# TensorE's values product put ahead of the transposes in each slot of a two-layer cross-attention kernel

## What is computed

```python
a = _layer_norm(audio_kv, ln_gamma, ln_beta)          # (8, 1500, 256)
Q = (hidden_states @ Wq.T).reshape(B, Tt, HEADS, HEAD_DIM).transpose(0, 2, 1, 3)
K = (a @ Wk.T).reshape(B, Ta, HEADS, HEAD_DIM).transpose(0, 2, 1, 3)
V = (a @ Wv.T).reshape(B, Ta, HEADS, HEAD_DIM).transpose(0, 2, 1, 3)
scores = jnp.einsum('bhtd,bhsd->bhts', Q, K) * scale
attn = jax.nn.softmax(scores, axis=-1)
out = jnp.einsum('bhts,bhsd->bhtd', attn, V)
```

## Time and profile before

| | |
|---|---|
| median of 3 runs | 1822.67 us (1819.48, 1822.67, 1823.98) |
| profiled execution's own time | 1822.74 us |
| its span, first to last instruction | 1820.9 us |
| mean granted TensorE clock (share of full speed) | 0.973 |
| first layer's slots | from about 60 us to 483 us |
| steady period of a batch of the first layer | 50.2 to 51.7 us |
| busy share of the span | PE 92%, DVE 67%, ACT 57%, POOL 49% |

### The profile page before, as it was taken

One profiled execution on the slowest core, in us unless ns is written; L12 is line 12 of the kernel. 1 busy time (PEld: TensorE's weight loads), 2 busy tenths in 40 slices (PEclk: granted clock), 3 DMA queues, 4 the chain that ended last, 5 costly groups with the idle time before them and its releaser, 6 DMA issues.

```text
span 1820.9 us, 40621 instructions
## 1 busy us (share of the span) xinstructions
PE 1671.2 (92%) x12520; PEld 1571.5 (86%) x12520; DVE 1214.3 (67%) x2334; ACT 1041.7 (57%) x2023; POOL 898.0 (49%) x655
## 2 busy tenths in 40 slices
PE   3698889887798999999999999989999999999997
PEld 2577777776688999999999997789999999999986
DVE  5477777766546667667766767466676676677673
ACT  2476666656454566565655656545565665656563
POOL 4455555533234365355445547544554653554483
PEclk8899999999889999999999999999999999999998
DMA  7766676775322111001101104221111010010021
GB/s 228 210 146 166 157 178 175 175 171 118 90 64 81 43 34 67 34 34 67 35 33 67 49 23 140 64 78 35 57 58 43 34 67 34 34 67 0 1 88 42
DMA packets 109911, 149.69 MB, mean 82 GB/s; under 512 B 25540, under 2 KB 95684, under 8 KB 109828
## 3 DMA queue, kind: packets, MB, share of 16 engines
q1 hardware_dynamic: 108484, 142.45, 28.0%
q10 hardware_dynamic: 1344, 6.19, 1.0%
HBM read 108.32 MB, written 3.42 MB: 61 GB/s over the span
## 4 chain that ended last, share of the span: by engine, by line
PE 63%; DVE 9%; SPq 6%; issue 4%; ACT 3%; DMA 2%; POOL 2%; DVEq 0%; ACTq 0%; POOLq 0%
PE ps L765 11%; PE ps L767 11%; PE ps L766 11%; PE ps L1016 7%; PE ps L1020 7%; PE ps L1018 7%; SPq L389 4%; PE ps L951 2%; DMA q<-q_scratch 2%; DVE ar L1851 1%; PE ps L996 1%; PE ps L983 1%; SPq L392 1%; DVE negm L1879 1%; ACT prob L1292 1%
## 5 line engine op out<-in xcount | busy, mean ns | idle before, releaser
L717 POOL TENSOR_TENSOR rr<-ar,rr 125x512 fp32r<-125x512 f32 x336 | 450.8, 1376 | 417.1 <-ACT rr L1474 401.1
L1016 PE MATMUL ps<-cx,rr 125*128 125x258 f32 x1344 | 395.5, 294 | 0.0
L1020 PE MATMUL ps<-cx,rr 125*128 125x258 f32 x1344 | 379.3, 282 | 0.0
L1018 PE MATMUL ps<-cx,rr 125*128 125x256 f32 x1344 | 379.2, 282 | 0.0
L765 PE MATMUL ps<-rr,ct 128*125 128x256 f32 x1152 | 330.6, 287 | 4.5 <-DVE ar L1896 2.7
L767 PE MATMUL ps<-rr,ct 128*125 128x256 f32 x1152 | 325.2, 282 | 0.0
L766 PE MATMUL ps<-rr,ct 128*125 128x256 f32 x1152 | 324.9, 282 | 0.0
L1018 PEld LDWEIGHTS ps<-cx,rr 125*128 125x128 f32 x1344 | 254.7, 190 | 0.0
L1020 PEld LDWEIGHTS ps<-cx,rr 125*128 125x128 f32 x1344 | 254.7, 190 | 0.0
L1016 PEld LDWEIGHTS ps<-cx,rr 125*128 125x128 f32 x1344 | 253.6, 189 | 0.1
L1461 ACT ACTIVATE ar<-ar 125x512 f32<-125x512 f32 x336 | 208.6, 626 | 78.2 <-DVE ar L1896 54.5
(11 more groups left out here) (210 smaller groups left out, 3743.2 us busy)
## 6 DMA issues: line engine op xcount, KB each, us to landing
raw_t<-in_ctx_t SPq DMA_DIRECT2D x24, 1500.0 KB, 6.3
k<-khl SPq DMA_DIRECT2D x192, 187.5 KB
raw<-in_ctx SPq DMA_DIRECT2D x16, 1500.0 KB
raw<-in_ctx SPq DMA_DIRECT2D x8, 1408.0 KB
raw<-stat_scratch ACTq DMA_DIRECT2D x7, 750.0 KB, 3.9
w_raw<-in_wq SPq DMA_DIRECT2D x32, 128.0 KB, 2.3
w_raw<-in_wk SPq DMA_DIRECT2D x32, 128.0 KB, 2.2
qo<-in_wqt SPq DMA_DIRECT2D x32, 128.0 KB, 2.4
```

Source lines behind the costliest of these rows:

```text
L717: pool.tensor_tensor(group(p[:, 1, :, :], u, k), x, f(group(p[:, 0, :, :], u, k)), ALU.subtract)\
L1016: pe.matmul(ps[:, bank, 0:D + 2], hi, cx[0:KC, c, 0:D + 2], start=c == 0, stop=False, skip_group_check=True)
L1018: pe.matmul(ps[:, bank, 0:D], hi, cx[0:KC, c, D + 2:CW], start=False, stop=False, skip_group_check=True)
L1020: mm = pe.matmul(ps[:, bank, 0:D + 2], lo, cx[0:KC, c, 0:D + 2], start=False, stop=c == CH - 1, skip_group_check=True)
```

## The change

In TensorE's `slot` the values block (step 7) goes ahead of the eight transposes (step 5) and of the statistics' transpose (step 6). The order becomes: scores, last third of the transposes, keys, weighted sum, **values, transposes, statistics**. Its waits move with it. No instruction is added or removed, and no other engine's stream changes.

```diff
                     weighted(b if t else b - 1, (t - 1) % SLOTS, g - 1, n if t else 1 - n)
-                transposes(g, t, 0)
-                transposes(g, t, 1)
-                if t == 3 and kind == "full":
-                    pe.wait_ge(s["zoc"], g)
-                    turn_stats(b + 2)
                 if t in V_AT and kind != "plain":
                     u = V_AT[t]
                     pe.wait_ge(s["zvl"], 6 * (b + 1) + u)
                     if t == 6 and later:
                         pe.wait_ge(s["zre"], b)
                     values(b + 1, u, 6)
+                transposes(g, t, 0)
+                transposes(g, t, 1)
+                if t == 3 and kind == "full":
+                    pe.wait_ge(s["zoc"], g)
+                    turn_stats(b + 2)
                 if t == 4 and later:
```

## The result

| | before | after |
|---|---|---|
| median of 17 runs | 1823.33 us | 1831.63 us |
| ratio, with its 95% interval | | 1.0045 (1.0028 to 1.0063) |
| profiled execution's own time, its span | 1822.74, 1820.9 us | 1832.52, 1830.7 us |
| mean granted TensorE clock | 0.973 | 0.971 |
| first layer ends (start of its output product) | 485.94 us | 493.82 us |

The change makes the kernel 8.3 us slower, by the medians. The forecast was 1831.0 us, 8.4 above the 1822.67 us that it started from.

What follows compares the result with a forecast made beforehand. TensorE, busy 88% of a first-layer batch, bounds beside a GpSimd and SP ring. Slot 3's -1.19 us and exposed waits sum to +1.68 a batch, +6.0 over five; with clock and later slots +8.4: 1831.0 us, range 1819 to 1838.

Steps and rivals of the forecast that it cites:

- The statistics' wait: Slot 3: the statistics' transpose no longer waits for GpSimd's power; 7.61 instead of 8.80 us, -1.19 us per full batch.
- The exposed chain: Slots 0, 1, 2: transposes, high split, low splits lose their cover; row maximum to row maximum 6.64 us: +0.72, +0.60, +0.42.
- second ring: Slots 0 to 2: the ring over bank 3, which the first low split frees for the next four transposes; 6.39 us.
- a 0.45 us wait of the four transposes: Sign in the profile after: in slots 0, 1, 2 and 7 the four transposes wait about 0.45 us for a low split.
- Slot 7: Slot 7: high split delayed behind ScalarE's rounding of the context; 6.88 us against 5.92, +0.96.
- Slots 4 and 5: Slot 4: weighted sum ends later, +0.48 us; slot 5: today's idle goes, -0.31 us.
- Five periods: Slot (0, 4) to (5, 4): five batches of 51.99 us, 259.95 instead of 253.93 us, +6.0.
- The cover in batch 6: Slots (5, 4) to (6, 4): ScalarE's 7.16 us idle for key copies swallows a 2.6 us loss; priced nothing.
- the clock's half: Five periods: half of the 1.55 us lost to a lower-clock stretch, added as 0.8 us because it may return.
- The gain wins: Rival: slots 7, 0, 1, 2 stay at 5.9 us, GpSimd's ring sets a 48.8 us period; 1815 us, chance 8%.
- It cancels: Rival: the exposed wait is about half of what was summed; 1824 us (1819 to 1828), chance 20%.
- The clock falls more often: Rival: TensorE's gaps in every slot bring the lower clock in every period; 1838 us, chance 12%.

Runs made afterwards that it cites:

- experiment 1: From the kernel before: values block ahead of the transposes in slot 3 alone, old order elsewhere; ratio 0.9971, median 1816.99 us.
- experiment 3: From the kernel before: only the statistics' transpose with its wait moved behind slot 3's values block; ratio 0.9959, median 1816.88 us.
- experiment 4: From the changed kernel: values block between the first four and second four transposes, statistics behind; ratio to the kernel before 1.0005, median 1824.80 us.
- experiment 5: From the changed kernel: VectorE's row maximum over one of three blocks of 500 scores; ratio to the kernel before 0.9953.
- experiment 6: From the kernel before: VectorE's row maximum over one of three blocks of 500 scores; ratio 1.0021.
- experiment 7: The kernel of experiment 3 with VectorE's row maximum over one of three blocks of 500 scores; ratio to the kernel before 0.995.
- 8: The kernel of experiment 3 with slot 6's values block ahead of its weighted sum; ratio to the kernel before 0.9932, median 1813.61 us.
- 2: From the kernel before: values ahead of the transposes in every slot with values but slot 3; ratio 1.0052, median 1834.15 us.

## Why the prediction was right, point by point

- **The statistics' wait.** Forecast: slot (4, 3) from 8.80 to 7.61 us, no wait at L775. Measured 7.62, no wait; in the others of batches 1 to 5 7.47 to 7.80. Experiments 1 and 3 show the gain by itself.
- **The exposed chain.** Forecast 6.64 us for slots 0, 1 and 2, from 0.58 + 0.58 + 1.16 behind the eight transposes; measured 6.67, 6.82, 6.66, with the same 0.58 and 0.58 in the rows above. Experiment 4 was worked out by the same pieces (6.4, measured 6.35). The second ring's 6.39 is seen in experiment 5 as 6.33. The forecast of a 0.45 us wait of the four transposes was half right: they start 0.47 later, but the bracket shows 0.23, because the tail of the scores (to 337.28) covers the rest.
- **Slot (4, 1)** is 0.18 us longer than forecast, and so is slot 1 of batches 1 to 3 (6.82 to 6.84); in batches 0, 5 and 6 it takes 6.65 to 6.67. In slot (4, 1) the values' first weights are loaded 0.22 us after the end of the split that they wait for, and the values start 0.25 after it:
```profile
294.52 0.68 DVE L1658 TENSOR_TENSOR v<-ps,v 128x512 fp32r<-128x512 f32 x1
...
295.12 2.05 DVE L1664 BATCH_NORM_STATS2 bn<-raw 128x6 f32<-128x256 f32 x6
295.42 0.19 PEld L765 LDWEIGHTS ps<-wv_s,ct 128*128 128x128 f32 x1 [0.29 <-issue]
```
  In slot (5, 1) the load comes 0.06 us after the split (347.45 against 347.39), as forecast, and VectorE's statistics run there too, so they are not the reason. What differs is the program around it: `whole_batches` runs batches 1 to 4 in a loop and has the others written out. In slot (4, 1) the trace has two of TensorE's waiting instructions between the split's end and the load (at 295.25 and 295.34); in slot (5, 1) such a one stands before the split's end, at 346.96. No run here was made for it.
- **Slot 7** was over-priced: 6.88 against 6.69. ScalarE's context block holds the high split back to 2.61 us into the slot (332.28 - 329.67), not 2.8, and the low split starts at 3.19, hardly later than the row maximum lets it.
- **Slots 4 and 5.** 5.58 and 5.15 against 5.64 and 5.33: the gain in slot 5 was put at 0.31 and is 0.13, over five periods the largest miss.
- **Slips in the working**, none of which moves the forecast by more than 0.3 us: slot 7's surplus is 3.38 - 3.16 = 0.22, not 0.24; its 0.58 + 0.95 + 1.97 make 3.50, not 3.4; and slots (5, 7) to (6, 2) lose 2.7 by the terms given, not 2.6.
- **Five periods**: 259.95 against 260.83 us. That they are so near is in part luck: over the five, slot 5 costs 1.1 us and slot 1 0.7 us more than forecast, slot 7 1.0 and slot 6 0.6 less.
- **The cover in batch 6.** From slot (5, 4) to (6, 4) 55.63 us instead of the earlier trace rows's 56.32, and ScalarE's idle time before the late keys falls from the 7.16 us of the earlier trace rows:
```profile
417.19 0.59 ACT L1238 ACTIVATE kst<-ps 128x500 f32<-128x500 f32 x1 [5.88 <-POOL khl L574]
```
  So the slots' loss there was hidden, as priced; the stretch is even 0.7 us shorter, which offsets most of the 0.9 us that the five periods take above the forecast. Why it is shorter was not looked into.
- **The sum.** The first layer ends 7.88 us later; the forecast without the clock's half was 7.6. The clock's 0.8 is not seen in the first layer. The profiled spans differ by 9.8 us, the medians by 8.3. At the second layer's LayerNorm near 1140 us the kernel after is 7.45 us behind (1147.77 against 1140.32), some 20 us later 9.83 us (1169.05 against 1159.22): there the clock is granted lower for longer. By stretch, 14 us of it, first in the kernel before, then in the kernel after:
```profile
1146.00:1160.00 14.00, 12.53 (x59) 10.94 (x59) 5.83 (x9) 4.75 (x8) 1.85 (x3) 0.76 0.06 17
```
```profile
1153.50:1167.50 14.00, 13.21 (x50) 11.68 (x51) 4.83 (x8) 3.35 (x6) 2.32 (x2) 0.58 0.00 1
```
  The change moves no instruction there; why the clock differs is open. So the total of 8.4 met the 8.3 by luck in its last 0.8 us: the term for the clock stands for no event of the changed kernel's first layer.
- **The rivals.** "The gain wins" needed four slots at 5.9 us; none is. That its ring exists is shown by experiments 3, 6 and 7. "It cancels" falls with the 6.67. "The clock falls more often": the profile after has full clock in all five periods. The new gaps in slots 0 to 2 are 0.2 to 0.3 us; slots 6 and 7 keep waits of 1.3 to 1.4 us, which did not bring it down there. The mean clock of the 17 executions after has a median of 0.973, the same as the profile before. In experiments 6 and 7 the clock fell behind waits of 1.7 to 4.2 us. The Trainium skill, "TensorE: Matmul & The Clock Gate", section "HAM oscillation — how this bites in real kernels", says that waits between bursts of matmuls bring the clock back to half. Its case has waits longer than the bursts between them. Experiments 6 and 7 agree in kind. The prediction's "by that rule this rival would hold" took the rule further, to gaps that are a small part of a slot, and the full clock behind gaps of 0.2 to 0.3 us does not bear it out. Why experiment 4 lost the clock in three slots 6 and the changed kernel in none is open.

## What to carry to other kernels

A block of independent matmuls is a cover, and moving it uncovers what it hid: before moving it, list what runs on the other engines during it, and add those durations behind the instruction that will now stand last. If one wait is to be covered, move the waiting instruction behind the cover (experiment 3, ratio 0.9959), not the cover ahead of everything (1.0045); the cover ahead in the one slot that waits (experiment 1, 0.9971) exposes one slot only and can't be told from experiment 3. Where two rings turn side by side, what one engine saves comes back as waits as soon as the other ring binds (experiment 6).

## What the hardware showed that was not expected

- After TensorE had waited 3.39 us in slot (3, 3) of experiment 6, its matmuls of 256 columns followed one another at 0.21 us instead of 0.12; the values block lost 1.2 us on top of the wait.
- The length of the wait alone does not decide. The stretch at the lower clock that the earlier trace rows show in one period lies in slot (1, 6). In order of time, the kernel before:
```profile
167.86 0.98 PE L864 MATMUL ps<-pt,v 128*66 128x224 f32 x4 [1.35 <-DVE pt L1658]
168.64 1.70 PE L847 MATMUL ps<-ident,prob 112*128 112x112 f32 x8
...
321.01 0.60 PE L864 MATMUL ps<-pt,v 128*66 128x224 f32 x4 [1.35 <-DVE pt L1658]
321.45 0.93 PE L847 MATMUL ps<-ident,prob 112*128 112x112 f32 x8
```
  Behind the same wait of 1.35 us the eight transposes last 1.70 us in slot (1, 6) and 0.93 in slot (4, 6). By stretch, the same kernel:
```profile
168.00:172.00 4.00, 4.00 (x24) 4.00 (x25) 1.67 (x4) 3.30 (x7) 1.15 (x3) 0.60 0.91 188
172.00:176.00 4.00, 2.77 (x24) 2.39 (x24) 2.85 (x3) 3.03 (x4) 4.00 (x2) 1.00 0.72 148
```
  The granted clock is 0.60 of full over the first 4 us, so most of them ran at the lower of its two levels, 1.2 GHz of 2.4, while TensorE worked throughout; it is full again in the next 4 us.
- Experiment 7 shows the same with longer waits. Its statistics' transposes in slots (2, 3) and (4, 3):
```profile
203.27 0.28 PE L775 MATMUL ps<-ident,mv 128*12 128x128 f32 x1 [1.69 <-POOL mv L580]
...
304.88 0.28 PE L775 MATMUL ps<-ident,mv 128*12 128x128 f32 x1 [2.73 <-POOL mv L580]
```
  Slot (2, 4), behind the shorter wait, takes 6.71 us at a mean clock of 0.75; slot (4, 4), behind the longer, 5.14 at 1.00.
- In batches 0 to 5 a slot 6 or 7 lost the clock once in the kernel before and in experiments 1, 3 and 5 each, twice in 8, three times in 4, and never in the changed kernel or in 2. These are single executions. What else sets off the fall stays open.
